# Two attention loops run as one chain, and an indexed fetch moved into the steps of a third

## The reference

```python
x = x + tanh(g_xattn[0]) * cross_attention(layernorm(x), ctx, ctx, Wq, Wk, Wv, Wo)      # 16 heads of 8
# second block, on z = layernorm(x); l = 0: token mixture of experts, l = 1: sequence mixture
for l in range(2):
    z = z + self_attention(ln(z) * ln1_w[l] + ln1_b[l], wq[l], wk[l], wv[l], wo[l], bq[l], bk[l], bv[l], bo[l])  # causal
    h = ln(z) * ln2_w[l] + ln2_b[l]
    cw = softmax over the two best of (h @ gate_w[l] + gate_b[l])     # two of eight experts
    z = z + sum over chosen experts e of cw[e] * (gelu(h @ w1[l, e] + b1) @ w2[l, e] + b2)
x = x + tanh(g_ffn[0]) * z_result
x = x + tanh(g_xattn[1]) * mlstm_cell(layernorm(x), ctx)              # gated linear attention, 8 heads of 16
x = x + tanh(g_ffn[1]) * int8_linear(layernorm(x))
# int8_linear: scale = max|x| / 127; clip(round(x / scale), -128, 127) @ W8.T * scale * weight_scale + bias
```

## Time and profile before

| | us |
|---|---|
| median of 3 runs (lowest to highest) | 1284.59 (1283.62 to 1286.57) |
| the profiled execution's own time | 1285.98 |
| its span, first to last instruction | 1284.2 |
| TensorE busy | 982.4 (76%) |
| VectorE busy | 860.2 (67%) |
| ScalarE busy | 675.5 (53%) |
| GpSimd busy | 587.5 (46%) |
| mean granted TensorE clock | 0.84 of full |

### The profile page before, as it was taken

One profiled execution on the slowest core, in us unless ns is written; L12 is line 12 of the kernel. 1 busy time (PEld: TensorE's weight loads), 2 busy tenths in 40 slices (PEclk: granted clock), 3 DMA queues, 4 the chain that ended last, 5 costly groups with the idle time before them and its releaser, 6 DMA issues.

```text
span 1284.2 us, 31133 instructions
## 1 busy us (share of the span) xinstructions
PE 982.4 (76%) x9819; PEld 765.4 (60%) x9833; DVE 860.2 (67%) x2083; ACT 675.5 (53%) x1713; POOL 587.5 (46%) x801
## 2 busy tenths in 40 slices
PE   2999983999975899995003999965999969799503
PEld 1677762777755889995001777744777749555301
DVE  3899966899965856663234899977222254389896
ACT  2777742777741067774002777753555522588503
POOL 3555572566610055553774666612333310378423
PEclk9999975999975589998555999985999995699855
DMA  4000130000002022222114000000000001011002
GB/s 120 16 15 14 47 98 1 2 0 0 1 1 66 1 58 66 67 67 49 53 51 144 2 0 0 1 1 0 0 0 0 0 25 50 7 47 44 28 0 65
DMA packets 48792, 38.66 MB, mean 30 GB/s; under 512 B 6024, under 2 KB 41332, under 8 KB 48740
## 3 DMA queue, kind: packets, MB, share of 16 engines
q1 hardware_dynamic: 41988, 27.74, 7.3%
q0 software_dynamic: 4320, 8.86, 2.7%
q10 hardware_dynamic: 2432, 1.40, 0.4%
HBM read 29.13 MB, written 8.85 MB: 30 GB/s over the span
## 4 chain that ended last, share of the span: by engine, by line
PE 61%; DVE 11%; issue 8%; POOL 7%; POOLq 6%; ACT 3%; DVEq 1%; DMA 1%; SPq 1%; ACTq 0%
PE ps_s L912 13%; PE ps_o L912 12%; PE ps_v L912 7%; PE ps_a L912 7%; PE ps_t L993 7%; PE ps_t L912 7%; POOLq L612 4%; POOL h_all L582 2%; POOL w L582 2%; PE ps_v L1013 2%; POOL work L613 2%; PE ps_x L948 2%; POOLq L602 1%; DVE stats L1286 1%; DVE inner_all L1368 1%
## 5 line engine op out<-in xcount | busy, mean ns | idle before, releaser
L558 POOL TENSOR_TENSOR kbd<-kts,kmask 128x512 f32<-128x512 f32 x192 | 240.7, 1276 | 229.7 <-ACT qts L716 146.9
L575 POOL DMA_INDIRECT xg<-x_rows,row_from x71 | 76.3, 1075 | 147.5 <-DVE slot_of L1506 84.9
L1328 DVE TENSOR_REDUCE rowmax<-ps_s 128x16 f32<-128x1024 f32 x96 | 116.4, 1213 | 21.9 <-PE ps_s L912 21.7
L738 ACT COPY probs_t<-ps_t 128x1024 f32<-128x1024 f32 x96 | 97.2, 1012 | 62.3 <-PE ps_t L993 62.3
L912 PE MATMUL ps_s<-kbd,qts 64*64 64x512 f32 (+1 forms) x1024 | 124.8, 559 | 1.1 <-issue 1.1
L1331 DVE TENSOR_TENSOR work<-ps_s,rowmax 128x1024 f32<-128x1024 f32 x96 | 117.5, 1224 | 3.3
L948 PE MATMUL ps_x<-ident,xn 128*128 128x128 f32 x96 | 31.2, 325 | 113.0 <-DVE xn L1319 113.0
L912 PE MATMUL ps_o<-vst,probs_t 128*64 128x18 f32 x3072 | 108.5, 214 | 7.5 <-ACT probs_t L738 7.5
L912 PEld LDWEIGHTS ps_o<-vst,probs_t 128*64 128x64 f32 x3072 | 98.9, 139 | 20.0 <-ACT probs_t L738 9.8
L993 PE MATMUL ps_t<-ident,work 128*128 128x128 f32 x768 | 102.0, 277 | 4.8 <-ACT work L730 4.8
L730 ACT ACTIVATE work<-work 128x1024 f32<-128x1024 f32 x96 | 101.0, 1052 | 2.6 <-DVE work L1331 2.5
(11 more groups left out here) (365 smaller groups left out, 2404.8 us busy)
## 6 DMA issues: line engine op xcount, KB each, us to landing
y_rows<-work SPq DMA_DIRECT2D x71, 64.0 KB, 1.6
w<-in_L_ffn_e_w_dram SPq DMA_DIRECT2D x2, 2048.0 KB, 9.3
ctx_dup<-in_ctx_dram SPq DMA_DIRECT2D x64, 64.0 KB, 2.2
ctx_in<-in_ctx_dram SPq DMA_DIRECT2D x32, 64.0 KB, 1.7
x_rows<-h_all SPq DMA_DIRECT2D x1, 2048.0 KB, 8.7
work<-in_ctx_dram SPq DMA_DIRECT2D x8, 256.0 KB, 2.8
out_dram<-work SPq DMA_DIRECT2D x16, 128.0 KB, 1.8
xg<-x_rows,row_from POOLq DMA_INDIRECT x71, 2.5
```

The source lines that it names most:

```text
L558: i = pool.tensor_tensor(km[:, par, g, :, :], kts[:, par, g:g + 1, :].to_broadcast([P, 8, SEQ]), kmask[:, :, :], ALU.mult)
L575: pool.indirect_dma_start(xg[:, t % XBUFS, :], None, x_d, bass.IndirectOffsetOnAxis(row_from[:, t:t + 1], 0)).then_inc(xg_loaded[t % XBUFS ...
L738: nc.scalar.copy(probs_t[:, par, :], ps_t[:, :]).then_inc(S["pts_ready"], 1)
L1328: V.tensor_reduce(rowmax[:, par, :], s3, AXX, ALU.max).then_inc(S["max_ready"], 1)
```

## The change

1. The cross-attention and the first self-attention run as one chain (`chained`): one stream of 64 tile steps, rolled into hardware loops except around the seam. Row statistics of the second part come in two groups (the first 20 tiles, then 12) as hooks between iterations.
2. The norm of the norm is closed: with variance v of x, the second factor is 1/sqrt(v (1 + eps) + eps^2), so xn of the first self-attention comes straight from x_res. The tile of inner that the residual needs is made by ScalarE in the loop (`inner_step`). `plain_norm` with its statistics goes.
3. `late_setup` is cut into pieces inside the cross-attention's first iterations. Only eight loads precede the first product, x comes in four pieces, and the other thirty loads and b2b are issued by SyncE before its third context load.
4. GpSimd makes the routing constants before the first loop and the others after the second.
5. Fetch, both adds and the statistics become steps of the second self-attention, whose own steps come LEAD = 12 iterations later; row statistics in groups of eight tiles as hooks; a ring of 16 semaphores for the fetches; xn moves to ScalarE. These loops are written out (`straight`) on VectorE, ScalarE and GpSimd.
6. At the end ScalarE does the norm tile by tile, VectorE's minimum and maximum and GpSimd's bias follow in quarters, and quantising is one operation in place of two.

```diff
+GROUP = 8
+NGROUP = NT // GROUP
+LEAD = GROUP + 4
+RING = 16
+def straight(steps, hooks=(), n=NT):
+    hooks = dict(hooks)
+    for i in range(n + max(step[0] for step in steps)):
+        if i in hooks:
+            hooks[i]()
+        for step in steps:
+            t = i - step[0]
+            if 0 <= t < n:
+                step[1](t, t % 2, *(t % buffers for buffers in step[2:]))
+def later(steps, lag):
+    return [(step[0] + lag,) + tuple(step[1:]) for step in steps if step]
+def chained(eng, segments, hooks=(), n=NT, unroll=4):
...
+        EARLY = 20
+        AT_MEANS, AT_ROOT, AT_RSTD = NT - 2, NT - 1, NT
+        AT_MEANS2, AT_ROOT2, AT_RSTD2 = NT + 7, NT + 8, NT + 9
# SyncE
-            sp.dma_start(x_res[:, :].rearrange("p (t d) -> p t d", d=D), x_v).then_inc(S["x_loaded"], 16)
+            for q in range(4):
+                a, b = q * (NT // 4), (q + 1) * (NT // 4)
+                sp.dma_start(x3[:, a:b, :], x_v[:, a:b, :]).then_inc(x_loaded[q], 16)
...
+                    if isinstance(t, int) and t == 2:
+                        late_loads()
...
-            sp.wait_ge(S["x_updated"], UPD[0] + NT + 2 * NT)
+            sp.wait_ge(S["second_done"], NT)
# GpSimd
+            def fetch(t, par):
+                seen(pool, S["second_done"], t - RING + 1)
                 for c, dst in enumerate((y_first, y_second)):
                     pool.indirect_dma_start(tile(dst, t), None, y_d, bass.IndirectOffsetOnAxis(slot_of[:, c, t:t + 1], 0)
-                                            ).then_inc(in_loaded[t // (NT // 4)], 16)
-            pipeline(pool, [(2, kbd_step(ATT["x"]))])
+                                            ).then_inc(fetched[t % RING], 16)
+            routing_constants()
+            chained(pool, [[(2, kbd_step(ATT["x"])), None], [(2, kbd_step(ATT[0])), (4, bias_step(0))]])
             other_constants()
-            pool.wait_ge(S["setup_copied"], 8)
-            pipeline(pool, [(2, kbd_step(ATT[0])), (3, bias_step(0))])
...
-            for t in range(NT):
-                fetch(t)
-            pipeline(pool, [(2, kbd_step(ATT[1])), (3, bias_step(1))])
+            straight(later([(2, kbd_step(ATT[1])), (3, bias_step(1))], LEAD) + [(0, fetch)])
# ScalarE
+            def inner_step(t, par):
+                nc.scalar.activation(tile(inner, t), tile(x_res, t), ACT.Identity, bias=nbias[:, bass.ds(t, 1)],
+                                     scale=rstd[:, bass.ds(t, 1)]).then_inc(S["inner_ready"], 1)
...
+                        (3, inner_step) if l == 0 else None, (L_SCORES, exp_step(base))]
+            chained(act, [attention("x", None), attention(0, 0)],
+                    {AT_ROOT: lambda: row_std(CH_EARLY, 0, EARLY, True), AT_ROOT2: lambda: row_std(CH_LATE, EARLY, NT, True)})
+            straight(later(attention(1, 1), LEAD) + [(LEAD, normalise)],
+                     {GROUP * g + LEAD - 1: lambda g=g: row_std(CH_SELF1 + g, GROUP * g, GROUP * (g + 1))
+                      for g in range(NGROUP)})
# TensorE
-            attention("x", None, CROSS)
-            late_setup()
-            attention(0, 0, SELF0)
+            chained(pe, [attention("x", None, CROSS), attention(0, 0, SELF0)])
# VectorE
+            def combine_first(t, par):
+                dve.wait_ge(fetched[t % RING], 32 * (t // RING + 1))
                 V.scalar_tensor_tensor(tile(inner, t), tile(y_first, t), tw1[:, t:t + 1], tile(inner, t),
-                                       ALU.mult, ALU.add).then_inc(S["x_updated"], 1)
+                                       ALU.mult, ALU.add).then_inc(S["first_done"], 1)
...
+                dve.wait_ge(S["late_loaded"], 16 * N_WLOADS)
...
-            for q in range(0, NT, 4):
-                dve.wait_ge(in_loaded[q // (NT // 4)], 16 * 2 * (NT // 4))
...
-            attention(1, inner, SELF1, 1.0)
+            for g in range(NGROUP):
+                a, b = GROUP * g, GROUP * (g + 1)
+                hooks[a + LEAD - 1] = lambda k=CH_SELF1 + g, a=a, b=b: row_means(k, b, a, b, False, "stats_done")
+                hooks[a + LEAD] = lambda k=CH_SELF1 + g, a=a, b=b: row_rstd(k, a, b, False, True)
+            attend = attention(1, inner, inner, SELF1, rstd, 1.0)
+            straight([(1, combine_first), (2, combine_second), (3, sums_step(inner, "second_done", 0, "stats_done"))]
+                     + later([attend[0]] + attend[2:], LEAD), hooks)
...
-            plain_norm(x_res, inner, NORM1, False)
-            V.tensor_reduce(xscale[:, 0:1], inner[:, :], AXX, ALU.min).then_inc(S["fin_link"], 1)
-            V.tensor_reduce(xscale[:, 1:2], inner[:, :], AXX, ALU.max).then_inc(S["fin_link"], 1)
+            for q in range(NCH):
+                dve.wait_ge(S["xn_ready"], NORM1 + (q + 1) * CHT)
...
-                V.tensor_scalar(qb[:, par, :], qa[:, par, :], 127.0, MAGIC, ALU.min, ALU.add).then_inc(S["qb_ready"], 1)
+                V.tensor_scalar(qb[:, par, :], inner[:, bass.ds(t * QW, QW)], xscale[:, 1:2], MAGIC, ALU.mult, ALU.add
+                                ).then_inc(S["qb_ready"], 1)
```

More of the change, by code:

```diff
@@ L30 @@
 QT = 2
+NCH = 4
+CHT = NT // NCH
 QW = QT * P
@@ L102, in pipeline, with at, rolled @@
                 call(step, i - step[0], i - step[0])
+SEAM = 4
+def straight(steps, hooks=(), n=NT):
[10 more added lines that the diff above has]
+def chained(eng, segments, hooks=(), n=NT, unroll=4):
+    hooks = dict(hooks)
+    count = len(segments[0])
+    lags = [max(seg[k][0] for seg in segments if seg[k]) for k in range(count)]
+    head = (max(lags) + unroll) // unroll * unroll
+    def at(i):
+        if i in hooks:
+            hooks[i]()
+        for k in range(count):
+            g = i - lags[k]
+            if 0 <= g < n * len(segments):
+                step = segments[g // n][k]
+                if step:
+                    step[1](g % n, g % 2, *(g % buffers for buffers in step[2:]))
+    def rolled(seg, begin, end):
+        with eng.Fori(begin // unroll, end // unroll, 1) as turn:
+            i0 = turn * unroll
+            for u in range(unroll):
+                for k in range(count):
+                    step = segments[seg][k]
+                    if step:
+                        j = u - lags[k]
+                        step[1](i0 + j, j % 2, *(j % buffers for buffers in step[2:]))
+    i = 0
+    for seg in range(len(segments)):
+        stop = seg * n + head + (SEAM if seg else 0)
+        while i < stop:
+            at(i)
+            i += 1
+        end = n - (SEAM if seg + 1 < len(segments) else 0)
+        rolled(seg, i - seg * n, end)
+        i = seg * n + end
+    while i < n * len(segments) + max(lags):
+        at(i)
+        i += 1
 def build(nc, A, out):
@@ L274, in build @@
         amax = sb("amax", [P, 1])
+        nbias = sb("nbias", [P, NT])
+        ends = sb("ends", [P, 2, NCH])
         amrow = sb("amrow", [1, P])
@@ L280, in build @@
         q8t = sb("q8t", [P, 2, QW], BF16)
-        qa, qb, o1, o3 = (work[:, k * 2 * QW:(k + 1) * 2 * QW].rearrange("p (b n) -> p b n", b=2) for k in range(4))
+        qb, o1, o3 = (work[:, k * 2 * QW:(k + 1) * 2 * QW].rearrange("p (b n) -> p b n", b=2) for k in range(3))
         ps_s = psum("ps_s", 1024)
@@ L666, in _ @@
         def _(act):
[L667 removed]
+            for dst, src in first_loads:
                 act.dma_start(dst, src).then_inc(S["weights_loaded"], 16)
[L669 removed]
             k = [0]
@@ L883, in _ @@
             nc.scalar.activation(gtmp[:, :, :], lsig[:, :, :], ACT.Sqrt, scale=1.0 / MHD).then_inc(S["gstd_ready"], 1)
-            row_std(7)
+            row_std(CH_NORM1)
+            act.wait_ge(S["nbias_ready"], 2 + NGROUP + 1)
+            for t in range(NT):
+                nc.scalar.activation(tile(inner, t), tile(x_res, t), ACT.Identity, bias=nbias[:, t:t + 1],
+                                     scale=rstd[:, t:t + 1]).then_inc(S["xn_ready"], 1)
             act.wait_ge(S["amrow_ps"], 1)
@@ L945, in fn @@
                 def fn(t, par):
+                    if base == "x" and isinstance(t, int):
+                        setup_piece(t)
                     pe.wait_ge(S["xn_ready"], nbase + t + 1)
@@ L1107, in _ @@
             pipeline(pe, [(1, turn_transpose, XBUFS), (3, turn_second, XBUFS), (1, turn_hidden)], NTURN)
-            attention(1, 1, SELF1)
+            pipeline(pe, [step for step in attention(1, 1, SELF1) if step])
             for g in range(NB):
@@ L1308, in row_stats, with row_rstd @@
+                V.tensor_scalar(vares[:, 0, c], var[:, c], EPS, None, ALU.add).then_inc(S["vare_ready"], 1)
                 assert n[0] == STAT_LINKS * (k + 1)
+            def row_rstd(k, a=0, b=NT, twice=False, bias=False):
+                n_, c = (2 if twice else 1), slice(a, b)
                 dve.wait_ge(S["std_ready"], k + 1)
-                V.reciprocal(rstd[:, :], std[:, :]).then_inc(S["rstd_ready"], 1)
+                V.reciprocal(rstds[:, 0:n_, c], stds[:, 0:n_, c]).then_inc(S["rstd_ready"], 1)
@@ L1541, in _ @@
+            for q in range(4):
```

(6 more changed lines are left out.)

304 lines of the change are left out of this document (162 added, 142 removed).

## The result

The changed kernel takes **1336.49 us** (median of four, 1334.51 to 1338.24); the kernel before took 1284.11 on the same chip (1279.88 to 1286.57). The ratio is 1.042, 95% interval 1.039 to 1.044: slower by 4.2%. The forecast was 1330 in 1299 to 1347.

What follows compares the result with a forecast made beforehand. The prediction saw gaps worth closing before the second self-attention (91 us without TensorE) and between the first two loops, but expected a ring of waits: 1286 - 1 (start) - 25 (seam) + 77 (ring) - 7 (end) = 1330 us, range 1299 to 1347.

Steps and rivals of the forecast that it cites:

- The ring: Second self-attention: kbd, bias, fetch, landing, adds, y, transposes, projection, copies, kbd close once per tile; 15 rings of 13.0 us, +77 us.
- the lead: Second self-attention: the attention's twelve-step lag behind the fetches doesn't open the ring, since both sides are shifted by it.
- The low-clock sum of 13.3: Second self-attention: ring length with TensorE at the low clock, 4.8 us from y to kbd in place of 2.95.
- The clock: TensorE in the second self-attention: waits over 4 us pull the granted clock below 1.0; ring 11.5 us full, 13.3 low.
- The 13.0: Second self-attention: ring length taken for the forecast, near the low-clock end; 15 x 13.0 = 195 us.
- rival 1: Second self-attention: the ring holds but TensorE keeps its full clock; 51 for 77, 1304 us; chance 0.17.
- Start of the rings and after: Second self-attention, from first fetch: kbd of tile 0 at 35.5, tile 3 at 58, tile 18 at 253, last at 317.
- The seam: First two attention loops chained: last cross-attention kbd to last first self-attention kbd 165.1 us instead of 190.5; -25 us (-19 to -40).
- rival 3: First two loops: chain saves little, ScalarE bounds the first self-attention at 5.0 a tile, late loads; +15, 1345 us; chance 0.09.
- The start: Kernel start: earlier small loads bring x's second transpose from 26.65 to near 24.2, setup gives 1.6 back; -1 us (-6 to +4).
- The end: Kernel end: normalisation to maximum 13.9 us instead of 17.1, quantising loop about 4 us less; -7 us (-4 to -10).
- the second: Second self-attention: the lead is real slack, GpSimd's own work sets 5.75 us a step; -38 for +77, 1215 us; chance 0.09.

Runs made afterwards that it cites:

- fetch_first: Changed kernel with GpSimd's fetch put ahead of the K product and bias in each step of the second self-attention; 1252.0 us, 0.973 of the kernel before.
- adds_later: Changed kernel with VectorE's two adds and sums two steps later and the lead 14 tiles instead of 12; 1249.7 us, 0.970 of the kernel before.
- lead20: Changed kernel with the attention 20 tiles behind the fetches instead of 12; 1296.0 us, 1.008 of the kernel before.
- keep_busy6: Changed kernel with six extra unused TensorE products after the scores of tiles 4 to 18 of the second self-attention; 1336.6 us, 1.035 of the kernel before.
- inner_last: Changed kernel with ScalarE's inner_step behind the exponentials in the first self-attention instead of ahead; 1330.9 us, 1.038 of the kernel before.
- out4: Changed kernel with four output buffers instead of two in the last, quantising and storing loop; 1329.3 us, 1.034 of the kernel before.
- best_c: best_a with GpSimd's fetch also ahead of the product in its step; 1216.5 us, 0.942 of the kernel before.
- adds_behind: Changed kernel with VectorE's adds and sums moved behind y and the row maxima in its step; 1252.3 us, 0.968 of the kernel before.
- best_a: Changed kernel with the edits of adds_behind, inner_last and out4 together; 1236.5 us, 0.957 of the kernel before.

## Why the prediction was right

**The ring** was derived from the step lists, and the runs bear out each part of it. It closes once per tile (fifteen steps of 12.61 on the mean), it runs through both GpSimd's and VectorE's order (each of fetch_first and adds_later opens it), and the lead does not open it (lead20). Its terms, forecast and measured in the rows above: kbd to the end of the bias 2.93, 2.92; to the first fetch 0.31, 0.14; to the second 1.26, 1.29; landing 2.53, 2.54; five VectorE operations 1.5, 1.30; from y to kbd, between 2.95 and 4.8, 4.47. The low-clock sum of 13.3 was 0.7 too high: 0.2 in the way to the first fetch, 0.2 in VectorE's five operations, 0.3 between y and kbd (1.71 from the transposes' start to the projection's and 2.44 from there to kbd, where 1.91 and 2.61 were taken).

**The clock** was the term with wide bounds. In all fifteen rings the transposes took 1.91 us as in the earlier trace rows, against 1.04 at full clock (2.4 GHz) in the earlier trace rows: after its wait for y TensorE is at the low level each time. Before that wait it varies. The scores took 1.03 us in eleven rings, as they do at a granted clock of 1.00 in keep_busy6, and 1.92 in four. One of each, from the timeline of the changed kernel:

```profile
702.85 1.03 PE L1035 MATMUL ps_s<-kbd,qts 64*64 64x512 f32 x8
...
716.39 1.92 PE L1035 MATMUL ps_s<-kbd,qts 64*64 64x512 f32 x8
```

The mean over the rings is 0.70. The Trainium skill's HAM oscillation ("TensorE: Matmul & The Clock Gate") says that bursts with waits between them keep falling to the low level; the trace agrees, in all fifteen rings. So the low-clock sum was the one that applied. The 13.0 that I took was a point between the two prices, and it came out nearer than 13.3 only because that sum was too high: this part is luck. keep_busy6 shows the full-clock ring of rival 1: 11.1 us, forecast 11.5. That rival was wrong about the clock and right about its price.

**Start of the rings and after.** First kbd 34.7 us after the first fetch (35.5), tile 3 at 56.9 (58), tile 18 at 246.1 (253), the last at 313.1 (317).

**The seam** of the first two loops was off by 5 us. From the last kbd of the cross-attention (173.94) to the last of the first self-attention (338.71) it is 164.8 us, where the forecast had 165.1; but the statistics and roots of the early tiles run before that kbd and cost 4.9 us there, which the sum had counted inside. Both groups together widen six gaps between kbd products by 11.4 us where 8 was taken, and ScalarE's new step costs 0.28 a tile, 8 to 9 us, where 0.22 and 7 were taken. inner_last shows that it is this step. The period of 4.97 is the one that rival 3 feared (5.0), and the chained loops save their time all the same.

**The start** gives nothing in the end. The first kbd comes at 19.78 and not near 27, the second transpose of x at 22.41 against 26.65, so this step was forecast too small (22.41 where 24.2 was forecast). But the following kbd gaps are 4.3 to 6.7 us, and the seventh kbd starts at 53.50 against 53.33 before: an early start is worth only what the next stage can take up. In seven of the other eleven variants the seventh kbd even starts 3.6 to 6.1 us later than before the change; why, no run shows.

**The end** is the term that was wrong in kind, -2.4 where -7 was forecast. The normalisation to the maximum took 15.3 us against 17.1 (forecast 13.9), since ScalarE's 32 operations take 12.42 us, 0.39 each and not 0.35. And the quantising loop was reckoned by its engines alone. Before, all but the last of GpSimd's adds waited for VectorE, at 1.45 us a double tile; with VectorE's operation gone they wait for the stores of two output buffers, at 1.44. So a gain of 4 us was forecast where a second bound lay just below the first, and out4 takes that one away.

Of the rivals, the second (slack in the lead, 5.75 us a step, 1215 us) describes the kernel one would have with an open ring, and best_c's step is 5.33. For the changed kernel itself lead20 refutes it.

## What to carry to other kernels

When work moves into a software-pipelined loop whose engines each keep a fixed order, follow one new transfer from its issue through every in-order engine back to the queue that issues it, and count the steps of the circle: the period is the circle's time divided by the number of steps it spans, or more if something else bounds it. A longer lead shifts both ends: here it left the period at 12.3 to 12.7 us and only made fewer steps pay it. A different place in one engine's list, or a larger lag between issue and use, shortens it. If no engine of a stage is the bottleneck (here the busiest had 59% of it) and each waits for the next, look for such a circle before looking for a slow engine.

## What the hardware showed that I had not expected

**VectorE waits for GpSimd's product.** In the timeline of the changed kernel small VectorE operations with two inputs in SBUF take 1.2 us beside kbd and 0.17 once it is over:

```profile
839.02 2.50 POOL L658 TENSOR_TENSOR kbd<-kts,kmask 128x512 f32<-128x512 f32 x2 [1.76 <-ACT qts L822]
839.10 1.22 DVE L1423 TENSOR_TENSOR half_gap<-stats 128x8 f32<-128x8 f32 x1
840.36 1.19 DVE L1424 TENSOR_TENSOR mean<-stats 128x8 f32<-128x8 f32 x1
...
842.19 0.17 DVE L1427 TENSOR_TENSOR var<-stats 128x8 f32<-128x8 f32 x1
```

1.2 us is one of the two products of kbd (1.275 us mean). The Trainium skill has the rule in "SBUF — State Buffer", SBUF: two separate sides: a port pair is shared by the two engines and held for a whole instruction, and a VectorE operation with two SBUF inputs needs it against a GpSimd operation that reads SBUF. The trace agrees: the first operation ends at 840.32, within 0.1 us of the end of kbd's first product, and the second with the second product. The prediction had not weighed it in the ring. In the closed ring it costs little, since the adds run while GpSimd is idle (0.35 us). In an opened ring they fall into the product. The timeline of fetch_first:

```profile
685.92 2.55 POOL L658 TENSOR_TENSOR kbd<-kts,kmask 128x512 f32<-128x512 f32 x2 [0.91 <-ACT qts L822]
...
686.59 0.75 DVE L1651 SCALAR_TENSOR_TENSOR inner_all<-h_all,tw,inner_all 128x128 f32<-128x128 f32 x1 [0.69 <-DMA w<-y_rows,slot_of]
687.26 1.35 DVE L1657 SCALAR_TENSOR_TENSOR inner_all<-w,tw,inner_all 128x128 f32<-128x128 f32 x1
...
688.54 0.28 DVE L1407 BATCH_NORM_STATS2 stats<-inner_all 128x6 f32<-128x128 f32 x1
...
689.01 0.29 DVE L1478 TENSOR_TENSOR y<-ps_o,recip 128x128 f32<-128x128 f32 x1
...
692.22 2.50 POOL L658 TENSOR_TENSOR kbd<-kts,kmask 128x512 f32<-128x512 f32 x2 [0.91 <-ACT qts L822]
```

The second add ends 0.14 us after the product, y starts 0.4 us behind it and the next kbd 2.9 behind the end of y: a second ring, kbd over the port to y and back, of 6.30 us. It closes in each of the eight steps of 6.30, also in those in which no add waits for a fetch (kbd at 659.21, 679.61, 717.23 and 737.61). best_c has the adds behind the row maxima, where GpSimd issues its transfers, and there they take 0.34 and 0.39; T falls from 227.8 to 210.3. That the port alone gives these 17 us is argued from the rows, as best_c also takes the adds out of y's way; no run separates the two.

**What stays open.** With the changed kernel's lead and GpSimd's order the first kbd of the second self-attention comes 34.7 us after the first fetch in four kernels and 39.6 in three (keep_busy6, adds_behind, best_a), and the first gaps of the cross-attention and those in the seam of the first two loops add up to more in some kernels than in others. In keep_busy6 the row that ends the stop names only "remote":

```profile
621.12 0.37 ACT L816 ACTIVATE kts<-ps_a,vec_t 128x128 f32<-128x128 f32 x1 [6.96 <-remote]
```

No experiment was made on it.
